# One megakernel of eight stages: layer-norm work of two causal attention stages moved to their beginnings

## The chip, the cores and the metric

One core of a Trainium2 chip. The metric is the device time of one execution in microseconds, from the first to the last instruction of the core and what lies around them; a measurement is the median of several executions. The kernel is one program of 24930 instructions.

## The reference

Four transformer layers on x of 4 sequences x 512 tokens x 128 channels, float32. Each half-layer is `x = x + f(layernorm(x))`:

- L0: gated linear attention; grouped routed experts with a shared expert.
- L1: attention with low-rank q and k factors (16 heads of 8 channels), softmax and a causal mask; routed experts.
- L2: a block whose weights are generated (`tanh(mix) * W + B`): layernorm with gain and bias, causal softmax attention (16 heads of 8), residual, layernorm, a GELU MLP; then a ternary feed-forward `h = silu(x w1 s1) * (x w2 s2)`, two GELU layers 512 to 512, and an output layer.
- L3: full attention (16 heads of 64); dispatched experts with capacity.

The parts that matter here:

```python
def _layernorm(x, axis=-1, eps=1e-05):
    m = jnp.mean(x, axis=axis, keepdims=True)
    v = jnp.var(x, axis=axis, keepdims=True)
    return (x - m) / jnp.sqrt(v + eps)

scores = jnp.einsum('bhqd,bhkd->bhqk', q, k) / float(HD) ** 0.5
scores = jnp.where(causal, scores, -10000.0)
attn = jax.nn.softmax(scores, axis=-1)
```

The L2 block is itself applied to the normalised x, so its residual `hs` is a normalised x too, and its attention normalises twice.

## The kernel before, in words

The residual x stays in SBUF as 16 tiles of 128 tokens x 128 channels. Each sequence is a chunk c (B = 4 chunks, TPC = 4 tiles each). The stages run one after the other, in the order 0 to 7, each in a block of its own; a stage writes out for each of the engines a list of instructions with semaphore waits. Stage 2 is `low_rank_attention` (L1), stage 4 `generated_block` (L2: `generated_attention`, then `generated_mlp`), stage 5 `ternary_ffn`, stage 6 `full_attention`. Projections are made in three matmuls from a high and a low part of weights and rows (fp32r), which add up to float32.

**Layer norm** (class `LayerNorm`) has these steps for a chunk: `stats_of` (VectorE, L200 and L203, 4 tiles each), `rstd_of` (GpSimd, L236 or L239 and the power at L242), `scaled_by` (L214, four tiles of 128x128, on VectorE or GpSimd), `turned` (TensorE, four transposes, L252), `copied` (ScalarE, a high part at L261 or L264 and the float32 copy at L266 or L268) and `low_part_by` (L224, VectorE or GpSimd). The scaled rows have two buffers, so chunk c waits until chunk c-2 was turned.

**The causal stages** (`causal_attention`, stages 2 and 4) work through 16 quads q, four per chunk; a quad is four heads in the four row groups of TensorE. A quad's steps: project q and k (`q`, `k`: L2303 to L2305), make their stacks (`q_stack`, `k_stack`: ScalarE L2418, VectorE L2482), 12 units of scores for the row maxima (`max`: TensorE L2323, VectorE L2502), the maxima turned (`maxT`, L2332) and subtracted (`less`, L2511), scores less the maxima in 6 parts (`exp`, L2344) with their exponentials (`exp_done`, ScalarE L2429 or L2432), a causal cut by GpSimd (L2270), products with the values (`pv`, L2358), and the quotient (`turn`, `norm`). Once a chunk: values (`v`, L2311; `v_done`, L2490) and output (`oT`, `y`). A list written out by hand, `TEMPLATE`, gives the order of one quad's period, with steps of several quads in it (the `pv` of a quad come two periods after its `max`); `causal_plan` unrolls it, and TensorE, ScalarE and VectorE each walk through the same plan and do their part of each item.

PSUM: `p1` two banks for the maxima, `p2` two double banks for the scores, `po` for the products with the values, and `pm`, a single bank, for all odd jobs: q, k, maxT, v, oT, y and, before, the turned rows of chunks 1 to 3 (`ln`). An odd job waits until the one ahead of it in the list was emptied.

**Before the change** a causal stage begins with chunk 0 alone: VectorE makes its statistics, scales its rows, and later makes the statistics of chunks 1 to 3. GpSimd clears the mask and the wide maxima right behind the first deviation (L2234 to L2237), clears the values' tile with its column of ones (L2240, L2242), and scales chunk 1. In the quads, GpSimd's queue holds the cuts of a quad and behind them, at fixed quads, the low part of the next chunk, the scaling of the one after it, and the output's bias added to the residual (L2252); in stage 4 ahead of this the normalised residual of the chunk (`make_hs`, L2616 to L2621). The item `("ln", c)` for chunks 1 to 3 stands behind the fourth unit of maxima of quad 4c-2.

**The ternary stage**: weights are split into 10 pieces of 128x512 (`SplitWeights`: high part on ScalarE, L301; low part on GpSimd, L306). GpSimd's queue: deviation of chunk 0, low part of piece 0, then pieces 1 to 5, then the deviation of chunk 1, then the low parts of the hidden rows. VectorE forms h0 = silu(a) * b in four steps f (L2089) with a high part each (L2082), and scales the next chunk's rows behind the first of them. TensorE's up-projection (L2006 to L2008) for step f waits for h0 of step f-2.

**The full attention stage**: GpSimd clears a tile for the maxima (L2846) and a tile of ones (L2848) around the first deviation.

## Time and profile before

| | us |
|---|---|
| median of 3 executions | 1692.11 |
| lowest and highest | 1687.55, 1694.02 |
| the profiled execution's own time | 1689.31 |
| its span, first to last instruction | 1687.6 |

The profile shows one execution. A row of the timeline gives start, duration, engine, line of the kernel, operation, what is written and read, the count, and in brackets the idle time of the engine before it and who ended it; rows with a count above 1 run several instructions of a kind together. PE is TensorE, PEld its weight loads, DVE VectorE, ACT ScalarE, POOL GpSimd. Rows of matmuls that overlap are pipelined.

Stages in the trace: stage 2 begins at 321 us and ends at 549, stage 4's attention goes from 642 to 868, the ternary stage from 906 to 1062, the full attention from 1062.

### The profile page before, as it was taken

Reading aid. Unit: us, or ns where it says so; the run is one execution under the profiler, and the core shown is the slowest. Engines: PE = TensorE matmul, PEld = TensorE weight load, DVE = VectorE, ACT = ScalarE, POOL = GpSimd, SP = SyncE. Lnnn points to the kernel's source line nnn. Section 1 sums busy time; section 2 is a strip of 40 time slices with the busy share of each in tenths; the row PEclk is TensorE's granted clock in tenths of the full one; section 3 lists DMA queues with packets and bytes.
Section 4 is the critical chain, followed back from the end, with each engine's and each line's share of the span. In section 5 each row is a group of like instructions: output and inputs, shape, how many; then the busy total and the mean of one; then the engine's idle time right before and its main releaser. Section 6 shows DMA issues by size and latency. Waiting matters only on the chain. (4 is left out here: it accounts for less than half of the span.)

```text
span 1687.6 us, 24930 instructions
## 1 busy us (share of the span) xinstructions
PE 1395.5 (83%) x8907; PEld 849.4 (50%) x8907; DVE 1042.6 (62%) x2864; ACT 747.3 (44%) x1169; POOL 763.4 (45%) x833
## 2 busy tenths in 40 slices
PE   5576688789998795999977999899999999985193
PEld 3354566644454562444435777555554545534062
DVE  5766678567884646688833222578778777757112
ACT  4554244336665341566644333455455454430041
POOL 5442344423432555354443442356555455563533
PEclk9688789859999796699978999799999999997597
DMA  3000004200000322000001020000000000003213
GB/s 97 7 8 1 34 22 193 85 1 1 1 2 1 129 63 97 1 2 1 2 0 53 1 100 1 1 1 1 1 1 1 1 1 1 1 1 125 63 51 100
DMA packets 29562, 52.74 MB, mean 31 GB/s; under 512 B 3216, under 2 KB 24592, under 8 KB 27264
## 3 DMA queue, kind: packets, MB, share of 16 engines
q1 hardware_dynamic: 26144, 44.36, 7.5%
q0 software_dynamic: 3296, 6.78, 1.2%
q8 instruction: 73, 1.20, 0.3%
q14 instruction: 49, 0.40, 0.1%
HBM read 29.07 MB, written 21.02 MB: 30 GB/s over the span
## 5 line engine op out<-in xcount | busy, mean ns | idle before, releaser
L2502 DVE CUSTOM_DVE_ANT_0 s_masked_scores<-s_for_max,s_mask_qk 128x128 bf16<-128x128 f32 (+3 forms) x512 | 227.0, 486 | 58.3 <-PE s_for_max L2323 56.4
L2863 POOL TENSOR_TENSOR wbuf<-s_probs 128x1024 f32<-128x1024 f32 x64 | 152.0, 2374 | 201.9 <-ACT s_probs L3022 201.9
L3022 ACT ACTIVATE s_probs<-s_scores 128x1024 f32<-128x1024 f32 x128 | 132.2, 1033 | 202.2 <-PE s_scores L2944 202.2
L2270 POOL TENSOR_SCALAR_AFFINE_SELECT s_probs<-s_probs 128x256 f32<-128x256 f32 x256 | 99.9, 407 | 247.7 <-ACT s_probs L2429 149.6
L3064 DVE TENSOR_REDUCE s_negmax<-s_for_max 128x2 f32<-128x1024 f32 x126 | 152.2, 1208 | 21.4 <-PE s_for_max L2919 21.3
L2323 PE MATMUL s_for_max<-s_k_stack,s_q_stack 32*128 32x128 f32 (+3 forms) x512 | 142.6, 441 | 26.9 <-DVE s_max_wide L2502 17.5
L3071 DVE RECIPROCAL s_recip<-s_pv_and_sums 128x128 f32<-128x128 f32 x128 | 116.6, 934 | 47.3 <-PE s_pv_and_sums L2970 47.3
L2323 PEld LDWEIGHTS s_for_max<-s_k_stack,s_q_stack 32*128 32x128 f32 x512 | 72.3, 205 | 128.8 <-DVE s_max_wide L2502 87.0
L2429 ACT ACTIVATE s_probs<-s_scores 128x1024 f32<-128x1024 f32 x128 | 127.4, 1024 | 14.0 <-PE s_scores L2344 13.7
L2957 PE MATMUL s_pv_and_sums<-s_probs,s_v 128*64 128x512 f32 x512 | 123.9, 605 | 0.9 <-DVE wbuf L3079 0.9
L2358 PE MATMUL s_pv<-s_probs,s_v_and_one 128*32 128x512 f32 (+3 forms) x1024 | 96.9, 474 | 1.5 <-DVE s_o L2521 1.5
L2418 ACT ACTIVATE s_low_rows_hi<-s_odd_jobs,s_low_rows_bias,s_low_rows 128x512 fp32r<-128x512 f32 x64 | 49.8, 777 | 106.9 <-PE s_odd_jobs L2305 106.9
L2344 PE MATMUL s_scores<-s_q_stack,s_k_stack 32*128 32x512 f32 (+3 forms) x512 | 81.8, 396 | 0.7 <-ACT s_probs L2429 0.7
L2868 POOL TENSOR_TENSOR xnT<-wbuf 128x1024 f32<-128x1024 f32 x32 | 78.1, 2442 | 2.5
L1986 POOL TENSOR_TENSOR s_h_lo<-s_h,s_h_hi 128x512 fp32r<-128x512 f32 x32 | 42.3, 1323 | 74.8 <-DVE s_h_hi L2082 74.8
L2944 PE MATMUL s_scores<-s_q_hi,s_k_hi 64*128 64x512 f32 x256 | 64.1, 497 | 9.6 <-ACT s_probs L3022 9.6
L1263 POOL TENSOR_TENSOR s_hidden_lo<-s_hidden,s_hidden_hi 128x512 fp32r<-128x512 f32 x36 | 46.4, 1290 | 46.3 <-ACT s_hidden_hi L1374 46.2
L2944 PEld LDWEIGHTS s_scores<-s_q_hi,s_k_hi 64*128 64x128 f32 x256 | 24.0, 184 | 77.2 <-issue 56.3
L2957 PEld LDWEIGHTS s_pv_and_sums<-s_probs,s_v 128*64 128x64 f32 x512 | 31.2, 136 | 61.4 <-issue 61.4
L2919 PE MATMUL s_for_max<-s_k_hi,s_q_hi 64*128 64x512 f32 x252 | 51.9, 407 | 0.8 <-ACT s_k_hi L2998 0.8
L3220 POOL DMA_INDIRECT expert_rows<-s_y,s_place_int x32 | 30.6, 957 | 47.4 <-DVE s_place_int L3429 37.3
L2944 PE MATMUL s_scores<-s_q_lo,s_k_hi 64*128 64x512 f32 x256 | 51.2, 395 | 0.0
(574 smaller groups left out, 3431.3 us busy)
## 6 DMA issues: line engine op xcount, KB each, us to landing
rows_by_expert<-s_empty_rows SPq DMA_DIRECT2D x8, 1032.0 KB, 10.5
s_w<-extra SPq DMA_DIRECT2D x2, 2048.0 KB, 10.1
wbuf<-w SPq DMA_DIRECT2D x1, 3460.0 KB, 11.2
s_generators<-extra SPq DMA_DIRECT2D x1, 2898.0 KB, 12.8
wbuf<-w SPq DMA_DIRECT2D x1, 2888.0 KB, 9.7
wbuf<-w SPq DMA_DIRECT2D x1, 2124.0 KB, 8.1
dispatched<-s_empty_slots SPq DMA_DIRECT2D x1, 2064.0 KB, 8.5
s_rows<-dispatched SPq DMA_DIRECT2D x8, 258.0 KB, 2.8
```

The lines of the kernel that those rows point to most:

```text
L2270: last = nc.gpsimd.affine_select(out=diag, in_=diag, compare_op=ALU.is_ge, fill=0.0, base=0, pattern=[[0, diag.shape[1]], [1, P]], channel ...
L2323: last = nc.tensor.matmul(p1[m % 2][:, at:at + n], stacks[0][rows, q % SLOTS, i * P:n], stacks[1][rows, q % SLOTS, 0:n], start=True, stop= ...
L2344: last = nc.tensor.matmul(p2[n % 2][:, at:at + S - j * P], stacks[1][rows, q % SLOTS, j * P:(j + 1) * P], stacks[0][rows, q % SLOTS, j * P ...
L2358: last = nc.tensor.matmul(po[32 * x:32 * x + 32, j * P:S], v32[:, c % 2, j, 4 * g + x, :], probs[:, q % 2, slab, at:at + S - j * P], start ...
L2429: nc.scalar.activation(probs[:, q % 2, r, :], p2[n % 2][:, :], ACT.Exp, scale=scale).then_inc(s_exp, 1)
L2502: last = nc.vector.tensor_tensor_reduce(out=junk[:, m % 2, at:at + n], in0=p1[m % 2][:, at:at + n], in1=mask[:, S - n:S], scale=1.0, scala ...
L2863: nc.gpsimd.tensor_tensor(added[half], probs[:, g % 2, 2 * half, :, :], probs[:, g % 2, 2 * half + 1, :, :], ALU.add).then_inc(s_added, 1)
L2944: last = nc.tensor.matmul(p2[:, x, :], kp, qp, start=(part == 0), stop=(part == 3))
L2957: last = nc.tensor.matmul(po[x * dh:(x + 1) * dh, :], v[:, c % 2, j, (2 * n + x) * dh:(2 * n + x + 1) * dh], probs[:, g % 2, j, x, :], sta ...
L3022: nc.scalar.activation(probs[:, g % 2, j, :, :], p2[:, :, :], ACT.Exp, scale=dh ** -0.5).then_inc(s_exp, 1)
L3064: nc.vector.tensor_reduce(negmax[:, g % 2, :, j], max_bank(g, j)[:, :, :], AX.X, ALU.max, negate=True).then_inc(s_neg, 1)
L3071: nc.vector.reciprocal(recip[:, at], ps_sum[:, at]).then_inc(s_rec, 1)
```

## The change

In both causal stages: the rows of all chunks are normalised in the beginning. VectorE makes the statistics of chunk 1 ahead of chunk 0's scaling, those of chunk 2 behind the biases and those of chunk 3 behind the low part of chunk 0. New items `("rows", c)` let VectorE scale chunk 1 ahead of the first q_stack and chunks 2 and 3 behind it. The `ln` items stand behind q(0), k(0) and max(0, 1), and turn into quarters of the score banks `p2` instead of the bank for odd jobs; the first two parts of the scores wait until these are copied out. GpSimd waits for chunk 0's scaled rows before it clears mask and maxima, and for the first two stacks before it clears the values' tile; behind that it makes the low parts of chunks 1 to 3, and adds the bias (stage 2: all chunks; stage 4: two chunks, with their residual). The rest of stage 4's residual is made in single steps, one a quad, behind the first cut of a quad. In the ternary stage the deviation of chunk 1 stands behind the second piece of the split weights. In the full attention stage the tile of ones is cleared ahead of the deviation.

```diff
--- before.py
+++ after.py
@@ -1968,7 +1968,9 @@
             pool.wait_ge(ln.s_xn, TPC)
             split.gpsimd(pool, range(1))
             pool.wait_ge(ln.s_lo, 1)
-            split.gpsimd(pool, range(1, 2 + n))
+            split.gpsimd(pool, range(1, 2))
+            ln.rstd_of(pool, 1)
+            split.gpsimd(pool, range(2, 2 + n))
             for c in range(B):
                 if c == 2 and clear:
                     nc.gpsimd.iota(empty_i[:, :], pattern=[[1, SLOTS7 // P]], base=T,
@@ -1976,7 +1978,7 @@
                     nc.gpsimd.memset(empty[:, :, 0:D], 0.0).then_inc(s_empty, 1)
                     pool.wait_ge(s_empty, 2)
                     nc.gpsimd.tensor_copy(empty[:, :, D], empty_i[:, :]).then_inc(s_empty, 1)
-                if c + 1 < B:
+                if c and c + 1 < B:
                     ln.rstd_of(pool, c + 1)
                 for i, h in enumerate((h0, h1)):
                     if c == 0 and i == 1:
@@ -2168,13 +2170,16 @@
         at = plan.index(item) + 1
         plan[at:at] = more
 
-    for c in range(1, B):
-        behind(("max", QUADS * c - 2, 3), ("ln", c))
+    plan.insert(plan.index(("q", 0)), ("rows", 1))
+    behind(("q", 0), ("ln", 1))
+    behind(("q_stack", 0), ("rows", 2), ("rows", 3))
+    behind(("k", 0), ("ln", 2))
+    behind(("max", 0, 1), ("ln", 3))
     return plan
 
 
 def causal_attention(sh, stage, ctx, ln, probs, p1, p2, po, pm, wst, qk_bias, s_wst, wv, wo, v_bias, o_bias, scale,
-                     before_scalar, before_vector, before_tensor, clear_gpsimd, hs=None, make_hs=None):
+                     before_scalar, before_vector, before_tensor, clear_gpsimd, hs=None, s_hs=None, make_hs=None):
 
 
 
@@ -2212,7 +2217,8 @@
     s_bias = sem("o_bias_added")
     SETUP = 6 + 4
     plan = causal_plan()
-    odd = [item for item in plan if item[0] in ("q", "k", "maxT", "v", "oT", "y", "ln")]
+    odd = [item for item in plan if item[0] in ("q", "k", "maxT", "v", "oT", "y")]
+    turned_in = [None, p2[0][:, 0:S], p2[0][:, S:2 * S], p2[1][:, 0:S]]
     block = ctx.enter_context(nc.Block())
 
     def emptied(item):
@@ -2220,7 +2226,7 @@
         what, n = item[0], item[1]
         if what in "qk":
             return s_stack, 2 * n + "qk".index(what) + 1
-        return {"maxT": s_sub, "v": s_v32, "oT": s_oTs, "y": s_x, "ln": ln.ready}[what], n + 1
+        return {"maxT": s_sub, "v": s_v32, "oT": s_oTs, "y": s_x}[what], n + 1
 
     @block.sync
     def _(sp):
@@ -2230,13 +2236,17 @@
     def _(pool):
         nc.gpsimd.iota(row[:, :], pattern=[[0, 1]], base=0, channel_multiplier=1).then_inc(s_row, 1)
         clear_gpsimd(pool)
-        ln.rstd_of(pool, 0)
+        for c in range(2):
+            ln.rstd_of(pool, c)
+        pool.wait_ge(ln.s_xn, TPC)
         nc.gpsimd.memset(mask[:, :], 0.0).then_inc(s_mask, 1)
         nc.gpsimd.memset(wide[:, :, :, :, :], 0.0).then_inc(s_wide, 1)
         pool.wait_ge(s_mask, 1)
         nc.gpsimd.affine_select(out=mask[:, S - P:], in_=mask[:, S - P:], compare_op=ALU.is_ge, fill=NEG,
                                 base=0, pattern=[[-1, P]], channel_multiplier=1).then_inc(s_mask, 1)
-        ln.rstd_of(pool, 1)
+        for c in range(2, B):
+            ln.rstd_of(pool, c)
+        pool.wait_ge(s_stack, 2)
         nc.gpsimd.memset(v32[:, :, :, :, HD8:32], 0.0).then_inc(s_ones, 1)
         pool.wait_ge(s_ones, 1)
         nc.gpsimd.memset(v32[:, :, :, :, HD8:HD8 + 1], 1.0).then_inc(s_ones, 1)
@@ -2244,18 +2254,21 @@
         resid = sh.x if hs is None else hs
 
         def add_bias(c):
-            if make_hs:
-                make_hs(pool, c)
-            else:
-                pool.wait_ge(ln.s_xn, (c + 1) * TPC)
+            pool.wait_ge(ln.s_xn if s_hs is None else s_hs, (c + 1) * TPC)
             ts = slice(c * TPC, (c + 1) * TPC)
             nc.gpsimd.tensor_tensor(resid[:, ts, :], resid[:, ts, :],
                                     o_bias.unsqueeze(1).broadcast_to([P, TPC, D]), ALU.add).then_inc(s_bias, 1)
 
-        ln.scaled_by(nc.gpsimd, pool, 1)
-        add_bias(0)
-        for c in range(2, B):
-            ln.rstd_of(pool, c)
+        for c in range(1, B):
+            ln.low_part_by(nc.gpsimd, pool, c)
+        if s_hs is None:
+            for c in range(B):
+                add_bias(c)
+        else:
+            for c in range(2):
+                for step in range(1 + TPC):
+                    make_hs(pool, c, step)
+                add_bias(c)
         for q in range(B * QUADS):
             for r in range(EXPS):
                 pool.wait_ge(s_exp, EXPS * q + r + 1)
@@ -2270,13 +2283,12 @@
                     last = nc.gpsimd.affine_select(out=diag, in_=diag, compare_op=ALU.is_ge, fill=0.0, base=0,
                                                    pattern=[[0, diag.shape[1]], [1, P]], channel_multiplier=-1)
                 last.then_inc(s_cut, 1)
-            c = q // QUADS + 1
-            if c < B and q % QUADS == 0:
-                ln.low_part_by(nc.gpsimd, pool, c)
-            if c + 1 < B and q % QUADS == 1:
-                ln.scaled_by(nc.gpsimd, pool, c + 1)
-            if c < B and q % QUADS == 2:
-                add_bias(c)
+                c, step = divmod(q - 1, 2 + TPC)
+                if s_hs is not None and r == 0 and 0 <= c < B - 2:
+                    if step <= TPC:
+                        make_hs(pool, c + 2, step)
+                    else:
+                        add_bias(c + 2)
         if hs is not None:
             for c in range(B):
                 ts = slice(c * TPC, (c + 1) * TPC)
@@ -2339,6 +2351,8 @@
                 pe.wait_ge(s_sub, q + 1)
             if n >= 2:
                 pe.wait_ge(s_exp, n - 1)
+            else:
+                pe.wait_ge(ln.ready, 3 + n)
             for x, j, at in score_units(r):
                 rows = slice(32 * x, 32 * x + 32)
                 last = nc.tensor.matmul(p2[n % 2][:, at:at + S - j * P], stacks[1][rows, q % SLOTS, j * P:(j + 1) * P],
@@ -2401,8 +2415,7 @@
             elif item[0] == "y":
                 project_out(item)
             elif item[0] == "ln":
-                odd_bank(item)
-                ln.turned(pe, item[1], pm)
+                ln.turned(pe, item[1], turned_in[item[1]])
 
     @block.scalar
     def _(act):
@@ -2418,7 +2431,7 @@
                 nc.scalar.activation(low[:, k, :], pm[:, :], ACT.Identity, bias=low_bias[:, k, g:g + 1],
                                      scale=sel[:, k:k + 1]).then_inc(s_low, 1)
             elif item[0] == "ln":
-                ln.copied(act, item[1], pm[:, :])
+                ln.copied(act, item[1], turned_in[item[1]])
             elif item[0] == "exp_done":
                 _, q, r = item
                 n = EXPS * q + r
@@ -2462,20 +2475,20 @@
                 st.did(nc.vector.tensor_scalar(low_bias[:, k, :], bias[:, k, :], sel[:, k:k + 1], None, ALU.mult))
             st.wait()
 
+        ln.stats_of(dve, 1)
         ln.scaled(dve, 0)
         dve.wait_ge(sh.wsem[stage], 16)
         set_bias()
         st.end()
+        ln.stats_of(dve, 2)
         before_vector(dve)
-        ln.stats_of(dve, 1)
         ln.low_part(dve, 0)
-        for c in range(2, B):
-            ln.stats_of(dve, c)
-        dve.wait_ge(s_mask, 2)
-        dve.wait_ge(s_wide, 1)
+        ln.stats_of(dve, 3)
         resid = sh.x if hs is None else hs
         for item in plan:
-            if item[0] in ("q_stack", "k_stack"):
+            if item[0] == "rows":
+                ln.scaled(dve, item[1])
+            elif item[0] in ("q_stack", "k_stack"):
                 q, k = item[1], "qk".index(item[0][0])
                 g = q % QUADS
                 dve.wait_ge(s_low, 2 * q + k + 1)
@@ -2494,6 +2507,9 @@
             elif item[0] == "max":
                 _, q, u = item
                 m = UNITS * q + u
+                if m == 0:
+                    dve.wait_ge(s_mask, 2)
+                    dve.wait_ge(s_wide, 1)
                 dve.wait_ge(s_max, m + 1)
                 if u == 0 and q >= 2:
                     dve.wait_ge(s_maxT, q - 1)
@@ -2610,24 +2626,25 @@
         def first_rows_scalar(act):
             ln.copied(act, 0)
 
-        def make_hs(pool, c):
+        def make_hs(pool, c, step):
             ts = slice(c * TPC, (c + 1) * TPC)
-            pool.wait_ge(ln.s_mv, (c + 1) * TPC)
-            nc.gpsimd.tensor_scalar(rstd[:, ts], ln.mv[:, ts, 1], LN_EPS, 1.0, ALU.add, ALU.mult).then_inc(s_once, 1)
-            pool.wait_ge(s_once, 2 * c + 1)
-            nc.gpsimd.tensor_tensor(rstd[:, ts], rstd[:, ts], sh.mhalf[:, ts], ALU.pow).then_inc(s_once, 1)
-            pool.wait_ge(s_once, 2 * c + 2)
-            for t in range(c * TPC, (c + 1) * TPC):
+            if step == 0:
+                pool.wait_ge(ln.s_mv, (c + 1) * TPC)
+                nc.gpsimd.tensor_scalar(rstd[:, ts], ln.mv[:, ts, 1], LN_EPS, 1.0, ALU.add, ALU.mult).then_inc(s_once, 1)
+                pool.wait_ge(s_once, 2 * c + 1)
+                nc.gpsimd.tensor_tensor(rstd[:, ts], rstd[:, ts], sh.mhalf[:, ts], ALU.pow).then_inc(s_once, 1)
+            else:
+                t = c * TPC + step - 1
+                pool.wait_ge(s_once, 2 * c + 2)
                 nc.gpsimd.tensor_scalar(sh.hs[:, t, :], sh.x[:, t, :], ln.mv[:, t, 0:1], rstd[:, t:t + 1],
                                         ALU.subtract, ALU.mult).then_inc(s_hs, 1)
-            pool.wait_ge(s_hs, (c + 1) * TPC)
 
         ca, cab = gen["ca_w"], gen["ca_b"]
         stacked = [[part[:, k, :, :, :].rearrange("p h r d -> p (h r d)") for part in wst] for k in range(2)]
         causal_attention(sh, stage, ctx, ln, probs, p1, p2, po, pm, stacked, cab[:, 0:2 * QUADS], s_wst,
                          ca[:, 2 * D:3 * D], gen["cp_w"], cab[:, 2 * QUADS:2 * QUADS + D], gen["cp_b"], HD8 ** -0.5,
                          first_rows_scalar, lambda dve: None, first_rows_tensor, lambda pool: None, hs=sh.hs,
-                         make_hs=make_hs)
+                         s_hs=s_hs, make_hs=make_hs)
 
 
 def generated_mlp(sh, stage, hid=512):
@@ -2844,8 +2861,8 @@
 
             pool.wait_ge(sh.wsem[stage], 16)
             nc.gpsimd.memset(negmax[:, :, :, :], 0.0).then_inc(s_const, 1)
+            nc.gpsimd.memset(ones[:, :], 1.0).then_inc(s_const, 1)
             ln.rstd_of(pool, 0)
-            nc.gpsimd.memset(ones[:, :], 1.0).then_inc(s_const, 1)
             pool.wait_ge(ln.s_xn, TPC)
             low_weights(0)
             pool.wait_ge(s_xlo, 1)
```

## Rows read from the trace of the kernel before

**Rows 1.** The page's first part: busy time, share of the span, instructions

```profile
PE 1395.5 (83%) x8907; PEld 849.4 (50%) x8907; DVE 1042.6 (62%) x2864; ACT 747.3 (44%) x1169; POOL 763.4 (45%) x833
```

**Rows 2.** Stretches: length, busy us (instructions) per engine, granted clock, DMA share, GB/s

```profile
321.47:386.32 64.85, 50.86 (x214) 30.87 (x214) 38.87 (x161) 19.25 (x25) 21.36 (x36) 0.50 0.14 56
642.32:703.76 61.44, 44.19 (x154) 24.05 (x158) 38.76 (x160) 19.33 (x24) 24.95 (x40) 0.50 0.12 49
918.80:922.21 3.41, 1.29 (x6) 0.72 (x4) 1.56 (x3) 1.12 (x2) 2.87 (x4) 1.00 0.00 0
922.21:932.46 10.25, 8.34 (x21) 6.33 (x22) 4.35 (x8) 5.12 (x8) 6.63 (x6) 0.50 0.01 2
```

**Rows 3.** Timeline of VectorE, the writes of k_stack: stage 2, then stage 4

```profile
339.25 0.75 DVE L2482 SCALAR_TENSOR_TENSOR s_k_stack<-s_odd_jobs,s_qk_bias,s_low_rows_hi 128x512 fp32r<-128x512 f32 x1 [2.55 <-ACT s_low_rows_hi L2418]
...
351.55 0.75 DVE L2482 SCALAR_TENSOR_TENSOR s_k_stack<-s_odd_jobs,s_qk_bias,s_low_rows_hi 128x512 fp32r<-128x512 f32 x1
...
403.69 0.74 DVE L2482 SCALAR_TENSOR_TENSOR s_k_stack<-s_odd_jobs,s_qk_bias,s_low_rows_hi 128x512 fp32r<-128x512 f32 x1
...
414.07 0.74 DVE L2482 SCALAR_TENSOR_TENSOR s_k_stack<-s_odd_jobs,s_qk_bias,s_low_rows_hi 128x512 fp32r<-128x512 f32 x1
...
426.56 0.75 DVE L2482 SCALAR_TENSOR_TENSOR s_k_stack<-s_odd_jobs,s_qk_bias,s_low_rows_hi 128x512 fp32r<-128x512 f32 x1
...
503.87 0.74 DVE L2482 SCALAR_TENSOR_TENSOR s_k_stack<-s_odd_jobs,s_qk_bias,s_low_rows_hi 128x512 fp32r<-128x512 f32 x1
...
514.87 0.75 DVE L2482 SCALAR_TENSOR_TENSOR s_k_stack<-s_odd_jobs,s_qk_bias,s_low_rows_hi 128x512 fp32r<-128x512 f32 x1
...
731.11 0.74 DVE L2482 SCALAR_TENSOR_TENSOR s_k_stack<-s_odd_jobs,s_qk_bias,s_low_rows_hi 128x512 fp32r<-128x512 f32 x1
...
743.97 0.75 DVE L2482 SCALAR_TENSOR_TENSOR s_k_stack<-s_odd_jobs,s_qk_bias,s_low_rows_hi 128x512 fp32r<-128x512 f32 x1
...
821.63 0.74 DVE L2482 SCALAR_TENSOR_TENSOR s_k_stack<-s_odd_jobs,s_qk_bias,s_low_rows_hi 128x512 fp32r<-128x512 f32 x1
...
832.63 0.74 DVE L2482 SCALAR_TENSOR_TENSOR s_k_stack<-s_odd_jobs,s_qk_bias,s_low_rows_hi 128x512 fp32r<-128x512 f32 x1
```

**Rows 4.** Timeline of TensorE, stage 2: turned rows of chunk 1, then first values products

```profile
368.13 1.12 PE L252 MATMUL s_odd_jobs<-ident,s_ln_xn 128*128 128x128 f32 x4
...
369.18 0.58 PE L2344 MATMUL s_scores<-s_q_stack,s_k_stack 32*128 32x256 f32 x2
...
370.50 2.05 PE L2311 MATMUL s_odd_jobs<-wbuf,xnT 128*128 128x128 f32 x8 [0.74 <-ACT xnT L268]
...
380.53 1.94 PE L2358 MATMUL s_pv<-s_probs,s_v_and_one 128*32 128x512 f32 x8
```

**Rows 5.** Timeline of VectorE, then TensorE, in the beginning of stage 2

```profile
331.46 0.86 DVE L200 BATCH_NORM_STATS2 s_ln_stats<-x_resid 128x6 f32<-128x128 f32 x4
...
332.51 0.66 DVE L224 TENSOR_TENSOR s_xnT_lo<-xnT,s_xnT_hi 128x512 fp32r<-128x512 f32 x1
...
335.95 0.75 DVE L2482 SCALAR_TENSOR_TENSOR s_q_stack<-s_odd_jobs,s_qk_bias,s_low_rows_hi 128x512 fp32r<-128x512 f32 x1 [0.69 <-ACT s_low_rows_hi L2418]
...
341.63 1.40 PE L2323 MATMUL s_for_max<-s_k_stack,s_q_stack 32*128 32x512 f32 x2 [0.79 <-DVE s_max_wide L2502]
```

**Rows 6.** Timeline of VectorE and GpSimd, beginning of stage 4: first rows and a clearing

```profile
645.05 1.92 DVE L214 TENSOR_SCALAR s_ln_xn<-x_resid,s_ln_mv,s_ln_rstd 128x128 f32<-128x128 f32 x4 [0.97 <-POOL s_ln_rstd L242]
...
645.38 0.94 POOL L2235 MEMSET s_max_wide<- 128x1024 f32 x1
```

**Rows 7.** Timeline of the ternary stage: VectorE, GpSimd, VectorE, TensorE

```profile
909.17 1.11 DVE L214 TENSOR_SCALAR s_ln_xn<-x_resid,s_ln_mv,s_ln_rstd 128x128 f32<-128x128 f32 x4 [1.42 <-POOL s_ln_rstd L242]
...
912.84 6.41 POOL L306 TENSOR_TENSOR s_w_lo<-wbuf,s_w_hi 128x512 fp32r<-128x512 f32 x5 [0.62 <-DVE s_xnT_lo L224]
...
920.64 2.05 DVE L214 TENSOR_SCALAR s_ln_xn<-x_resid,s_ln_mv,s_ln_rstd 128x128 f32<-128x128 f32 x4 [2.53 <-POOL s_ln_rstd L242]
...
923.41 0.79 PE L2006 MATMUL s_a<-s_xnT_hi,s_w_hi 128*128 128x512 f32 x1 [3.31 <-DVE s_h L2089]
```

## The prediction

> **What bounds the kernel now.** I read the page first. TensorE is busy for 83% of the span, VectorE for 62% [rows 1], but no engine is busy throughout, so what the change is worth has to be read where it works: the beginnings of the two causal stages (stage 2 from 321 us, stage 4 from 642 us), their quads, and the first chunk of the ternary stage (906 to 935 us).
>
> Then the table of stretches with the granted clock. Both causal stages run their first 64.9 and 61.4 us at 0.50, which is 1.2 GHz, and everything behind that at full clock [rows 2]. TensorE's activity is thin there: 50.9 of 64.9 us, with idle gaps at every handover. The reader should see that each matmul or transpose on the path costs about twice as much in the beginning as later.
>
> Then the timeline of VectorE, cut down to one instruction per quad, the write of k_stack. From one to the next is the period of a quad. A plain quad takes 10.38 us (403.69 to 414.07). A quad that holds a chunk's values and the next chunk's turned rows takes 12.49 us (414.07 to 426.56). The last quad with values has no turned rows behind it and takes 11.00 us (503.87 to 514.87). In stage 4 the same two are 12.86 and 11.00 us [rows 3]. So a chunk of turned rows in mid-plan costs 1.49 us in stage 2 and 1.86 us in stage 4. The reason is the one bank for odd jobs: transposes, ScalarE's two copies out, then the values, then the next projection, all in a line. VectorE sits idle for that line, since it can't take the values before they are made.
>
> **The change, part by part.** No instruction is added or dropped. GpSimd's 24 scalings of 128x128 in the two causal stages become VectorE's, and the rest is order, banks and waits.
>
> *Turned rows out of the quads.* For chunks 2 and 3 the gain is read off directly: 2 x 1.49 = 3.0 us in stage 2, 2 x 1.86 = 3.7 us in stage 4. Chunk 1 stands in the filling of the pipe, at the low clock. There the transposes begin at 368.13, the scores behind them at 369.18, and the values' matmuls at 370.50, after waiting 0.74 us for ScalarE's copy [rows 4]. Without the transposes the scores (0.58 us) start at 368.13 and the values at 368.7: 1.8 us earlier. In stage 4 the copies carry scale and bias and are longer; I add the difference of the later quads, 0.37 us: 2.2 us. Sum of this part: 4.8 + 5.9 = 10.7 us. What is late next is the chain every plain quad has, and the 11.00 us quads show its price, so I expect no new wait. Bounds: all of it, or half of the filling's share, if something else ends last there: 8.7 to 10.7.
>
> *The new beginning, stage 2.* Before, VectorE made the statistics of chunk 1 at 331.46, between the low weights and the low part of chunk 0, which came at 332.51 [rows 5]. After, they are made while it waits for the first deviation, so the low part starts 1.05 us earlier. Behind it stood two sets of statistics; now one set and four scaled rows stand there. A set is about 1.1 us, four rows alone are 1.11 us [rows 7], so q_stack still comes with its 0.69 us to spare [rows 5]. The other eight rows, 2.2 us, go into VectorE's 2.55 us of idle time before k_stack [rows 3]. If that cover were gone, 0.3 us per set would show. TensorE's transposes of chunk 1 and 2 fall into its waits for the stacks. Those of chunk 3 stand between the second and third unit of scores for the maxima, where TensorE is idle 0.79 us [rows 5]; four transposes are 1.12 us [rows 4], so some 0.4 us shows. Stage 2's beginning: 1.0 - 0.4 = 0.6 us gained.
>
> *The new beginning, stage 4.* There are no weights to split, so the low part waits for ScalarE's copies, and these for the first four rows. These took 1.92 us beside GpSimd's clearings (0.94 us for the wide maxima alone) [rows 6], where four rows alone take 1.11 [rows 7]. The clearings now wait for the rows: up to 0.8 us gained. Against it, chunk 1's statistics now precede the rows (about 1.1 us in a gap of 0.97 us [rows 6]: 0.2 us lost), and the clearings fall on the small bias steps and the next statistics, which may hand everything back. Bounds -0.2 to +0.6; I take 0.2, less the 0.4 us of chunk 3's transposes: -0.2.
>
> *GpSimd.* Its queue now stops for chunk 0's rows (behind it: mask, wide maxima, deviations 2 and 3) and for the first two stacks (behind it: the ones column, three low parts, the bias, in stage 4 the normalised residual of two chunks). Who needs them: VectorE's rows 2, the first maxima, the values some 30 us later, the cuts of the first probabilities. GpSimd is busy 21.4 of 64.9 and 25.0 of 61.4 us there [rows 2], so I cost this at nothing; if the cuts came late, the first values product would wait. In stage 4 the residual's steps now stand behind the first cut of a quad; the product that needs the cuts comes a quad later. Nothing.
>
> *Ternary stage.* Five split weights of GpSimd fill 912.84 to 919.25, then comes the second deviation, and VectorE's four rows start only at 920.64, after 2.53 us of idle time [rows 7]; its next gated product is late and TensorE stands still 3.31 us until 923.41 [rows 7]. After: the second weight ends at 914.1, the deviation takes 1.39 us (919.25 to 920.64), the other four weights then end at 916.8, 918.1, 919.4 and 920.6 (1.28 us each). VectorE comes at 918.1, in the midst of them. The rows of stage 4 show that a scaling waits for the GpSimd instruction that is running, but also that two in flight came through behind it (four took 1.92, not one per instruction). So two rows behind 919.4 and two behind 920.6: done at 920.8 instead of 922.69, gain 1.9 us. Bounds: 0.3 if each row waits for an instruction of its own, 3.5 if none waits (918.1 and 1.11 us). The Trainium skill, "SBUF — State Buffer", in "SBUF: two separate sides", says the pair of ports that VectorE and GpSimd share is locked for a whole instruction and the other engine fully blocks. By that rule the lower bound is the one to take, if turns are strict; the rows of stage 4 agree with the blocking and not with strict turns.
>
> *The clock there.* It was high for 3.41 us, of which TensorE worked 1.29 us, then low for 10.25 us with 8.34 us of work [rows 2]. With a gap of 1.4 us in place of 3.3 us I expect it to stay up. The 8.34 us would halve, 4.2 us at most; I take 3.5. Ternary stage: 5.4 us (0.3 to 7.7).
>
> *Last attention stage.* One clearing of 128x64 moves ahead of a deviation that waits for VectorE anyway. Nothing.
>
> **Sum.** Stage 2: 0.6 + 4.8 = 5.4. Stage 4: 5.9 - 0.2 = 5.7. Ternary: 5.4. Together 16.5 us, of an execution of 1689.31 us (span 1687.6): 1672.8. That execution is 2.8 us under the median of 1692.11, so against the median it is 1675.6, 1.0% faster. I say 1675.5.
>
> **Rivals.**
> 1. *The scaled rows take turns with the split weights* in the ternary stage. Speaks for it: 1.92 us in place of 1.11 [rows 6, 7]. Then 0.3 us are left there and the clock falls as before: 11.4 us in all, 1680.7.
> 2. *The low clock ends earlier in the fillings,* since the transposes thicken TensorE's beginning and the gap behind them goes. A quad takes 12.30 us at the low clock (339.25 to 351.55) and 10.38 at the high [rows 3]; one quad fewer in each stage is 3.8 us, with the forecast 1671.7; two quads 1668. Against: in stage 2 it rose at 386.32 [rows 2], 5.8 us after the first values products began (380.53 [rows 4]), the densest work so far.
> 3. *The low clock lasts longer.* The place is the same: TensorE has less work in the quads that used to raise the clock. Each further quad costs 1.9 us. From nine further quads in the two stages together the gain of 16.5 is eaten, and from fourteen it is slower by over 0.5%: 1702. Against: the dense products begin the same number of quads in, and the clock rose at once behind them.
> 4. *The rows delay the first stacks.* VectorE runs in order; if eight rows took 3.8 us like the blocked ones of stage 4, k_stack would slip by 1.3 us in both stages: 1678.1.
>
> **How the numbers follow.** Forecast 0.5, rival 1 0.22, rival 2 0.1, rival 4 0.1, rival 3 0.03, and 0.05 that the mid-plan gain is only partly there (1684 to 1690). A measurement of this kernel can tell about 0.5% (8.5 us) from no change: faster is below 1683.7. The forecast, rivals 1, 2 and 4 lie there, but rival 1 together with rival 4 and the scatter of the runs (1687.55 to 1694.02) reaches the bound, so faster 0.84, same 0.13, slower 0.03. The range goes from two quads of earlier clock (1668) to rivals 1 and 4 together (1683.3), widened below and above by little: 1667 to 1684.
>
> **What would show it.** The k_stack periods: no 12.49 or 12.86 left, 11.00 in their place, plain quads 10.38 as now. k_stack of quad 0 about 1 us earlier after stage 2's beginning, and about as late as now in stage 4. In the ternary stage TensorE's gap of 3.31 us under 1.5, and the clock at 1.00 from there on. Wrong would be: a wait of VectorE's q_stack or k_stack on nothing but its own rows, values products waiting for GpSimd, or periods above 10.4 in plain quads.

## The result and the profile after

| | us |
|---|---|
| before, median of 8 executions (lowest, highest) | 1689.06 (1684.88, 1694.02) |
| after, median of 8 executions (lowest, highest) | 1677.76 (1671.32, 1682.32) |
| ratio after to before | 0.9925, 95% interval 0.9904 to 0.9946 |
| the profiled execution of after: own time, span | 1678.31, 1676.4 |

The changed kernel is faster, by 0.5 to 1.0%. The same program was timed twice more: 0.9891 (0.9863 to 0.992) and 0.9913 (0.9888 to 0.9937). My 1675.5 against 1692.11 is a ratio of 0.9902, which lies in the second and third interval and a little below the first. The total was about right; what it is made of was not.

The page's first part after the change (columns as in [rows 1]):

```profile
PE 1402.2 (84%) x8907; PEld 853.4 (51%) x8907; DVE 1051.3 (63%) x2888; ACT 749.4 (45%) x1169; POOL 745.6 (44%) x809
```

24 instructions went from GpSimd (833 before) to VectorE (2864 before); the other engines have as many as before.

Where the time went, by stage. A stage is counted from its first statistics to the next stage's.

| us | stages 0, 1 | 2 | 3 | 4, attention | 4, MLP | 5, ternary | 6 | 7 |
|---|---|---|---|---|---|---|---|---|
| before | 313.3 | 227.8 | 92.9 | 226.1 | 38.1 | 156.1 | 469.3 | 155.6 |
| after | 313.5 | 221.1 | 92.7 | 222.7 | 38.1 | 156.0 | 469.1 | 156.1 |

The whole gain is in the two causal stages: 6.7 and 3.4 us. The ternary stage gave 0.1 us. (Another 1.5 us lie ahead of the first statistics, in the first loads: 8.4 and 7.0 us. A further trace of the kernel before has 7.6 there, and the changed kernel's other two have 8.4 and 7.9, so that is scatter.)

*The quads.* VectorE's writes of k_stack after, stage 2 and then stage 4, where before had [rows 3]:

```profile
399.18 0.75 DVE L2495 SCALAR_TENSOR_TENSOR s_k_stack<-s_odd_jobs,s_qk_bias,s_low_rows_hi 128x512 fp32r<-128x512 f32 x1
409.54 0.74 DVE L2495 SCALAR_TENSOR_TENSOR s_k_stack<-s_odd_jobs,s_qk_bias,s_low_rows_hi 128x512 fp32r<-128x512 f32 x1
420.54 0.74 DVE L2495 SCALAR_TENSOR_TENSOR s_k_stack<-s_odd_jobs,s_qk_bias,s_low_rows_hi 128x512 fp32r<-128x512 f32 x1
...
709.26 0.74 DVE L2495 SCALAR_TENSOR_TENSOR s_k_stack<-s_odd_jobs,s_qk_bias,s_low_rows_hi 128x512 fp32r<-128x512 f32 x1
721.14 0.74 DVE L2495 SCALAR_TENSOR_TENSOR s_k_stack<-s_odd_jobs,s_qk_bias,s_low_rows_hi 128x512 fp32r<-128x512 f32 x1
732.15 0.75 DVE L2495 SCALAR_TENSOR_TENSOR s_k_stack<-s_odd_jobs,s_qk_bias,s_low_rows_hi 128x512 fp32r<-128x512 f32 x1
```

The plain quad is 10.36 us as before, and the quad with values is now 11.00 us in both stages (409.54 to 420.54, 721.14 to 732.15), where it was 12.49 and 12.86. But 709.26 to 721.14 is a plain quad of 11.88 us. The stretches with their granted clock show why (columns as in [rows 2]; the last two follow on each other):

```profile
320.06:381.50 61.44, 51.54 (x222) 32.18 (x222) 43.00 (x174) 21.61 (x29) 24.13 (x37) 0.50 0.15 59
634.09:692.11 58.02, 45.09 (x162) 25.39 (x166) 41.14 (x172) 22.27 (x28) 31.99 (x47) 0.50 0.13 52
705.99:709.40 3.41, 2.80 (x21) 1.53 (x22) 3.38 (x17) 2.63 (x5) 1.60 (x3) 1.00 0.01 2
709.40:712.81 3.41, 3.41 (x19) 1.38 (x18) 1.70 (x6) 2.08 (x3) 1.17 (x3) 0.50 0.00 0
```

The two fillings still run at 0.50, for 61.4 and 58.0 us instead of 64.9 and 61.4. Then, in the midst of the quads, the granted clock is 1.2 GHz again for 3.41 us, and that quad is 1.5 us longer. I call this a dip. TensorE is busy for all of it, but that is no sign of denser work: its matmuls take longer at the low clock. In the 3.41 us ahead of the dip it had worked 2.80 us. A second one fell into stage 4's last quad with values (12.42 instead of 11.00 us).

*The filling of stage 2.* TensorE after, the place of [rows 4]:

```profile
365.08 0.87 PE L2335 MATMUL s_for_max<-s_k_stack,s_q_stack 32*128 32x512 f32 x2
365.17 0.58 PE L2358 MATMUL s_scores<-s_q_stack,s_k_stack 32*128 32x256 f32 x2
366.02 2.05 PE L2323 MATMUL s_odd_jobs<-wbuf,xnT 128*128 128x128 f32 x8
```

Scores, beside the scores for the maxima (L2335), then at once the values (L2323), with no transposes and no wait of 0.74 us for a copy. TensorE before, the row just ahead of [rows 4]:

```profile
367.28 0.87 PE L2323 MATMUL s_for_max<-s_k_stack,s_q_stack 32*128 32x512 f32 x2
```

*The beginning of stage 2.* VectorE, then GpSimd and TensorE:

```profile
330.19 0.68 DVE L224 TENSOR_TENSOR s_xnT_lo<-xnT,s_xnT_hi 128x512 fp32r<-128x512 f32 x1
...
333.55 0.75 DVE L2495 SCALAR_TENSOR_TENSOR s_q_stack<-s_odd_jobs,s_qk_bias,s_low_rows_hi 128x512 fp32r<-128x512 f32 x1 [0.61 <-ACT s_low_rows_hi L2431]
334.22 2.13 DVE L214 TENSOR_SCALAR s_ln_xn<-x_resid,s_ln_mv,s_ln_rstd 128x128 f32<-128x128 f32 x8
336.86 0.75 DVE L2495 SCALAR_TENSOR_TENSOR s_k_stack<-s_odd_jobs,s_qk_bias,s_low_rows_hi 128x512 fp32r<-128x512 f32 x1 [0.51 <-ACT s_low_rows_hi L2431]
...
337.67 2.66 POOL L2250 MEMSET s_v_and_one<- 128x3072 f32 x1 [4.35 <-DVE s_k_stack L2495]
...
338.39 1.11 PE L252 MATMUL s_scores<-ident,s_ln_xn 128*128 128x128 f32 x4
```

Both stacks still wait for ScalarE (0.61 and 0.51 us), so the rows are hidden. The eight rows of chunks 2 and 3 take 2.13 us in the gap ahead of k_stack. Chunk 3's transposes (L252) start at 338.39, behind the first scores for the maxima. GpSimd stands still 4.35 us until the stacks are written and then clears for 2.66 us.

*The beginning of stage 4*:

```profile
637.11 1.08 DVE L214 TENSOR_SCALAR s_ln_xn<-x_resid,s_ln_mv,s_ln_rstd 128x128 f32<-128x128 f32 x4
...
638.52 0.55 POOL L2242 MEMSET s_mask_qk<- 128x512 f32 x1
639.01 0.97 POOL L2243 MEMSET s_max_wide<- 128x1024 f32 x1
```

The first rows take 1.08 us instead of 1.92 [rows 6], and the clearings come behind them.

*The ternary stage.* VectorE, its rows by form (shortest, median, longest in ns), GpSimd, TensorE:

```profile
906.74 4.02 DVE L214 TENSOR_SCALAR s_ln_xn<-x_resid,s_ln_mv,s_ln_rstd 128x128 f32<-128x128 f32 x4
...
L214 DVE TENSOR_SCALAR s_ln_xn<-x_resid,s_ln_mv,s_ln_rstd x4: 335/1304/1316, 906.7 to 910.4; 128x128 f32<-128x128 f32 x4
...
904.02 5.18 POOL L306 TENSOR_TENSOR s_w_lo<-wbuf,s_w_hi 128x512 fp32r<-128x512 f32 x4
...
911.48 0.80 PE L2008 MATMUL s_a<-s_xnT_hi,s_w_hi 128*128 128x512 f32 x1 [2.83 <-DVE s_h L2091]
```

The rows start right behind the first step, without the 2.53 us of idle time, as wanted, but take 4.02 us instead of 2.05 [rows 7]: three of them 1.3 us each, one behind each of GpSimd's subtractions, the fourth 0.34. TensorE's gap is 2.83 us, from 3.31. And the clock:

```profile
897.13:907.37 10.24, 6.95 (x18) 5.23 (x19) 5.89 (x20) 5.42 (x9) 8.22 (x8) 0.50 0.57 212
907.37:910.78 3.41, 1.27 (x6) 0.69 (x4) 3.41 (x5) 1.07 (x2) 3.05 (x3) 1.00 0.00 0
910.78:921.02 10.24, 8.83 (x22) 6.69 (x23) 3.86 (x6) 5.12 (x8) 7.12 (x6) 0.50 0.01 2
```

Up for 3.4 us, in which TensorE worked 1.27, then down for 10.24 us: the picture of [rows 2].

### The profile page after: what moved, and what is told of

It is laid out like the page before. It is cut to its first block and busy times, and to the rows that moved or that the text cites. A ratio compares the mean times of both kernels' runs of the same rounds, so it can differ in the third digit from the quotient of the medians.

```text
span 1676.4 us, 24921 instructions
## 1 busy us (share of the span) xinstructions
PE 1402.2 (84%) x8907; PEld 853.4 (51%) x8907; DVE 1051.3 (63%) x2888; ACT 749.4 (45%) x1169; POOL 745.6 (44%) x809
## 5 line engine op out<-in xcount | busy, mean ns | idle before, releaser
L2335 PE MATMUL s_for_max<-s_k_stack,s_q_stack 32*128 32x128 f32 (+3 forms) x512 | 143.4, 446 | 23.6 <-DVE s_max_wide L2518 16.0
L2335 PEld LDWEIGHTS s_for_max<-s_k_stack,s_q_stack 32*128 32x128 f32 x512 | 72.5, 206 | 126.0 <-DVE s_max_wide L2518 85.5
L2974 PEld LDWEIGHTS s_pv_and_sums<-s_probs,s_v 128*64 128x64 f32 x512 | 31.2, 136 | 61.4 <-issue 61.4
```

The source lines that it names most:

```text
L2335: last = nc.tensor.matmul(p1[m % 2][:, at:at + n], stacks[0][rows, q % SLOTS, i * P:n], stacks[1][rows, q % SLOTS, 0:n], start=True, stop= ...
L2974: last = nc.tensor.matmul(po[x * dh:(x + 1) * dh, :], v[:, c % 2, j, (2 * n + x) * dh:(2 * n + x + 1) * dh], probs[:, g % 2, j, x, :], sta ...
```

## The experiments

In the first set each part was put into the kernel before by itself (e1, e2), the ternary stage's blocking was taken away (e3), and the changed kernel ran again (e4).

**e1** and **e2**, the parts alone. e1 is the kernel before with this, and e2 the kernel after without it:

```diff
-            split.gpsimd(pool, range(1, 2 + n))
+            split.gpsimd(pool, range(1, 2))
+            ln.rstd_of(pool, 1)
+            split.gpsimd(pool, range(2, 2 + n))
...
-                if c + 1 < B:
+                if c and c + 1 < B:
```

> The kernel before with the ternary stage's part of the change alone. Forecast's theory: 1.9 us from the rows and 3.5 us from the clock, about 5.4 us faster than the kernel before (0.3%). Theory of turns (each scaled row waits for one whole GpSimd subtraction, as the changed kernel's trace shows with three rows of 1.31 us): 0.1 to 0.5 us, which no timing tells from nothing; the trace has three long rows, a gap of TensorE of about 2.8 us, and the clock falls as before. If the ternary part only looked idle in one profile by chance, the times would differ by several us.

> The changed kernel with the ternary stage as before. Theory of turns: the whole gain of about 0.7% stays here, ratio to the kernel before 0.992 to 0.994. Forecast's theory: the ternary part carried a third, so the ratio would be about 0.9955. In the trace the steady quads of both causal stages are 10.37 us, those with values 11.00, with or without the two dips of the clock that the changed kernel's stage 4 had; dips at other quads, or none, speak for chance, dips at the same two quads for a cause in the plan.

Measured: e1 0.9985 (0.997 to 0.9999), e2 0.988 (0.9853 to 0.9906). So the causal part makes the gain. The ternary part by itself gave 0.2 to 5.1 us, by its interval little or nothing, and the forecast's 5.4 lies just outside it. In e1 the rows took 4.01 us in the same turns. Its stage 5 was 153.2 us all the same, 2.9 below before, since the low clock behind the gap lasted 3.4 us in this trace and not 10.2. Against that stand two dips in stage 4, with the old causal plan (quads of 11.89 and 11.85 us). e2's stage 2 took 221.3 us and its stage 4 220.1, without a dip.

**e3**, early rows that nothing blocks. Chunk 1's rows stand ahead of the first step, and GpSimd holds pieces 2 to 5 back until they are written:

```diff
             ln.rstd_of(pool, 1)
+            pool.wait_ge(ln.s_xn, 2 * TPC)
             split.gpsimd(pool, range(2, 2 + n))
...
             ln.stats_of(dve, 1)
+            ln.scaled(dve, 1)
...
-                    if f == 0 and c + 1 < B:
+                    if f == 0 and c and c + 1 < B:
```

> The changed kernel, but VectorE scales chunk 1 of the ternary stage ahead of h0(0), and GpSimd holds pieces 2 to 5 of the split weights until these rows are done. Theory of turns: the rows take 1.1 us in VectorE's idle time, h0(1) then waits for ScalarE alone, TensorE's gap of 2.83 us shrinks to about 0.5 us; 2.5 to 3 us gained from that against the changed kernel. If a short gap keeps the clock up, 3 us more, 5 to 6 us in all. Rival: the clock falls all the same, or pieces 4 and 5 become late and the first hidden layer waits for GpSimd instead: under 2 us.

**e4**, the kernel after:

> The changed kernel once more, for a second trace. Theory: the two dips of the clock in stage 4 (quads of 11.88 and 12.42 us) come from where the chip's clock decisions fall against the thin part of a quad, so they sit elsewhere or are missing, and spans differ by 1.5 us per dip. Rival: stage 4's changed queue of GpSimd delays something at these quads; then they come again at the same quads.

Measured: e3 0.9897 (0.9876 to 0.9919), span 1668.7; e4 0.9891, span 1672.7. By time the two can't be told apart. The traces can: e3's rows took 1.11 us, its clock stayed at 1.00 behind the first 10.24 us, and stage 5 took 151.2 us. In e4 the rows took the same 4.02 us as in after, and yet the clock stayed up in this execution. TensorE's gap and the stretches in e4:

```profile
910.45 0.50 PE L2008 MATMUL s_a<-s_xnT_hi,s_w_hi 128*128 128x512 f32 x1 [3.08 <-DVE s_h L2091]
```

```profile
905.79:909.20 3.41, 1.59 (x7) 0.94 (x5) 3.41 (x4) 1.38 (x2) 3.41 (x3) 1.00 0.00 0
909.20:919.40 10.20, 7.82 (x35) 6.26 (x36) 4.92 (x9) 5.70 (x9) 7.93 (x7) 1.00 0.01 2
```

The stage took 152.5 us where after took 156.0. In the same stretch behind the first 10.24 us at the low clock, TensorE had worked 1.59 us here and 1.27 us in after. The same program thus has both outcomes, and the clock alone is worth 3.5 us here. Rows without turns add 1.3 us to that (152.5 to 151.2).

The second set has one trace each of four kernels and no interval. **e5**, the kernel before:

> The kernel before once more, for a second trace. If the clock's falls in quads and in the ternary stage are a matter of where its decisions fall, then this trace differs from the first in such places: a quad of 11.8 to 11.9 us somewhere, or the ternary stage at another length than 156.1 us, with nothing changed in the program. Rival: stage lengths repeat within 0.3 us, and the changed kernel's differences of 3 us are the change's.

Measured: span 1685.7, no dip, every quad's period of [rows 3] within 0.02 us, stage 5 156.0 us.

**e6**, GpSimd's clearings without their two waits:

```diff
-        pool.wait_ge(ln.s_xn, TPC)
...
-        pool.wait_ge(s_stack, 2)
```

> The changed kernel without GpSimd's two new waits (chunk 0's scaled rows, first two stacks), so that its clearings stand where they did. Theory: they block VectorE's scaling again: first four rows of stage 4 about 1.9 us instead of 1.1, its k_stack(0) 0.6 to 1 us later counted from the first statistics; stage 2 nearly the same, since its weights end last, unless the column of ones (2.7 us) falls on the rows of chunk 1 and delays q_stack by up to 2 us. Rival: the new order alone carries the gain and the waits carry nothing: both stages unchanged within 0.2 us.

Measured: first rows unchanged (1.08 us in both stages): the deviation of chunk 1, which the change put ahead of the clearings, keeps GpSimd busy until VectorE is done, so the first wait costs and saves nothing. The second one matters. VectorE in stage 2 of e6, then GpSimd:

```profile
333.35 4.38 DVE L214 TENSOR_SCALAR s_ln_xn<-x_resid,s_ln_mv,s_ln_rstd 128x128 f32<-128x128 f32 x8
337.65 0.73 DVE L2493 SCALAR_TENSOR_TENSOR s_k_stack<-s_odd_jobs,s_qk_bias,s_low_rows_hi 128x512 fp32r<-128x512 f32 x1
...
332.39 2.66 POOL L2248 MEMSET s_v_and_one<- 128x3072 f32 x1
335.11 0.35 POOL L2250 MEMSET s_v_and_one<- 128x128 f32 x1
335.34 1.28 POOL L224 TENSOR_TENSOR s_xnT_lo<-xnT,s_xnT_hi 128x512 fp32r<-128x512 f32 x1
```

Eight rows take 4.38 us beside the clearings and the low part behind them instead of 2.13, k_stack waits for them instead of for ScalarE, and comes 1.66 us later than in after (18.01 against 16.34 us from the stage's first statistics), in stage 4 1.89 us later. That is my rival 4, and the wait on the two stacks is what prevents it.

**e7**, chunk 3's turned rows back in mid-plan, in the bank for odd jobs, behind the fourth maxima of quad 10, and GpSimd's low part of it (in lines not shown) behind the first cut of quad 9:

```diff
-    behind(("max", 0, 1), ("ln", 3))
+    behind(("max", QUADS * 3 - 2, 3), ("ln", 3))
```

> The changed kernel with chunk 3's turned rows back in mid-plan in the bank for odd jobs (its scaling stays in the beginning, its low part goes behind the first cut of quad 9). Theory: one quad of each stage, from k_stack 10 to 11, takes 12.49 and 12.86 us again instead of 11.00, 1.5 + 1.9 us longer; k_stack 0 to 1 goes from 12.49 back to 12.30. Rival: the cost in mid-plan came from GpSimd's scaling and bias in its queue and not from the bank: then it stays near 11.0.

Measured, k_stack in stage 4 of e7 around that quad:

```profile
762.86 0.75 DVE L2499 SCALAR_TENSOR_TENSOR s_k_stack<-s_odd_jobs,s_qk_bias,s_low_rows_hi 128x512 fp32r<-128x512 f32 x1
775.72 0.75 DVE L2499 SCALAR_TENSOR_TENSOR s_k_stack<-s_odd_jobs,s_qk_bias,s_low_rows_hi 128x512 fp32r<-128x512 f32 x1
```

12.86 us again, and 12.49 in stage 2 with a dip of 1.24 on top (13.73). The other quads with values stay at 11.00. So each 1.49 and 1.86 us belongs to its own chunk's transposes. The first quad's period, where chunk 3's transposes had stood, hardly moved: 12.46 and 12.44 in the two stages instead of 12.49 and 12.50, and 12.30 before. I had costed those transposes at 0.4 us; they cost 0.04.

**e8**, the statistics back behind the first rows (chunk 1 behind the weights, chunk 2 behind the low part of chunk 0; GpSimd's deviation of chunk 1, not shown, goes back behind the mask):

```diff
-        ln.stats_of(dve, 1)
         ln.scaled(dve, 0)
         dve.wait_ge(sh.wsem[stage], 16)
         set_bias()
         st.end()
-        ln.stats_of(dve, 2)
         before_vector(dve)
+        ln.stats_of(dve, 1)
         ln.low_part(dve, 0)
+        ln.stats_of(dve, 2)
         ln.stats_of(dve, 3)
```

> The changed kernel with the statistics of chunks 1 and 2 back behind the weights (chunk 1 ahead of chunk 0's low part, chunk 2 behind it). Theory: in stage 2 the low part and k_stack(0) come 1.0 to 1.1 us later, and with two sets of statistics and four rows before q_stack another 0.4 to 1.1 us; in stage 4 chunk 1's statistics fall in a wait, so 0.4 to 1.1 us from the second set only, less 0.2 us since the first rows start earlier. Rival: other things end last there and nothing moves by more than 0.3 us.

Measured, VectorE in stage 2 of e8, then of e3, which has the changed kernel's causal stages:

```profile
329.53 0.66 DVE L224 TENSOR_TENSOR s_xnT_lo<-xnT,s_xnT_hi 128x512 fp32r<-128x512 f32 x1
...
333.20 0.74 DVE L2494 SCALAR_TENSOR_TENSOR s_q_stack<-s_odd_jobs,s_qk_bias,s_low_rows_hi 128x512 fp32r<-128x512 f32 x1
...
320.69 0.87 DVE L200 BATCH_NORM_STATS2 s_ln_stats<-x_resid 128x6 f32<-128x128 f32 x4 [0.32 <-PEq L1173]
...
329.09 0.68 DVE L224 TENSOR_TENSOR s_xnT_lo<-xnT,s_xnT_hi 128x512 fp32r<-128x512 f32 x1
...
332.44 0.75 DVE L2497 SCALAR_TENSOR_TENSOR s_q_stack<-s_odd_jobs,s_qk_bias,s_low_rows_hi 128x512 fp32r<-128x512 f32 x1 [0.62 <-ACT s_low_rows_hi L2433]
```

From the low part to q_stack it is 3.67 us instead of 3.36, and q_stack no longer waits for ScalarE: with two sets of statistics in front, four rows don't fit. q_stack came 0.2 us late in both stages (13.25 against 13.03 us from the first statistics, 9.54 against 9.31). The low part itself was not later than in after (9.58 against 9.68), but the clocks differ: it fell 1.40 us behind the first statistics in e8 and 0.23 us ahead of them in after. In e3 it fell 1.45 us behind them, as in e8 but for 0.05 us, and there the low part came at 8.40, q_stack at 11.75 and k_stack at 15.06 us, against 9.58, 13.25 and 16.54 in e8. So with the clock alike, the statistics' new place is worth 1.18 us at the low part, where I had 1.05, and 1.5 us at both stacks.

The third set asked whether e3's clock was luck, and whether the early place or the held GpSimd made it. **e9** is e3 again, **e10** the kernel after, **e11** is e9 without `pool.wait_ge(ln.s_xn, 2 * TPC)`:

> The kernel of e3 a second time: chunk 1's rows of the ternary stage scaled ahead of the first h0, GpSimd holding its pieces back until they are done. Theory (the clock there goes by TensorE's gap, and rows that nobody blocks close it): rows about 1.1 us, no TensorE gap over 1.5 us up to the second chunk, granted clock 1.00 behind it, stage 5 about 151 us instead of 152.5 to 156; against the kernel after on the same chip 1.5 to 4.5 us faster, which is 0.1 to 0.3% and at the edge of what timing can tell. Rival (chance: the clock is drawn anew in each execution, and e3 had a lucky one): low clock in the stage again, 155 to 156 us, and timing equal to the kernel after.

> The changed kernel again, beside e9. Stage 5 at 156 us (low clock behind the gap of 2.8 us) or near 152.5 (high); both have been seen, and this says only how often. Rows of chunk 1 take strict turns with the split pieces again (three of 1.31 us). Zero to two clock dips of 3.4 us in the causal quads, 1.5 us each. Span 1671 to 1678.

> e9 without GpSimd's wait: the rows still stand ahead of the first h0, but GpSimd's pieces 2 to 5 run on beside them. If turns are strict, the rows take 3 x 1.31 + 0.33 = 4.3 us again, the first h0 comes about 2 to 3 us later than in e9 and the stage loses what the early place gave: stage 5 at 153 us or more, with a gap of TensorE ahead of the gated product. If what helped in e3 was the early place alone, stage 5 is near 151 as in e3.

Measured: e9 0.9898 (0.9877 to 0.9919), e10 0.9913 (0.9888 to 0.9937), e11 0.9901 (0.9874 to 0.9929). Stage 5: 151.3, 156.0 and 153.7 us. The stretches of e9, and then of e11:

```profile
900.27:910.51 10.24, 6.67 (x17) 5.06 (x18) 6.46 (x23) 5.13 (x9) 6.99 (x7) 0.51 0.57 212
910.51:920.80 10.29, 7.87 (x33) 5.41 (x32) 4.47 (x7) 7.06 (x11) 10.29 (x9) 1.00 0.01 2
```

```profile
906.69:910.10 3.41, 0.62 (x3) 0.50 (x3) 3.38 (x5) 0.69 (x1) 2.13 (x3) 0.99 0.00 0
910.10:913.51 3.41, 3.41 (x9) 2.62 (x9) 2.09 (x3) 0.69 (x1) 2.51 (x2) 0.51 0.02 5
```

And the rows with GpSimd's pieces in e11, by form and in the timeline:

```profile
L214 DVE TENSOR_SCALAR s_ln_xn<-x_resid,s_ln_mv,s_ln_rstd x4: 1300/1303/1321, 903.9 to 907.5; 128x128 f32<-128x128 f32 x4
...
903.79 4.97 POOL L306 TENSOR_TENSOR s_w_lo<-wbuf,s_w_hi 128x512 fp32r<-128x512 f32 x4
```

Four rows, four pieces, one row to a piece: 1.30 us each instead of some 0.28. The early place without the hold thus only moves the gap (TensorE stands 2.79 us ahead of the gated product), and the clock falls behind it. With the hold it did not, in either of two traces. In the timing these kernels overlap with the changed one, so I don't claim a better version; the traces say that e3's order is worth 1.3 to 4.8 us of its stage.

## Why the prediction was right, and where it was not

| us | forecast | measured in the traces |
|---|---|---|
| stage 2, beginning | 0.6 | 1.2 (1.9 where the clock fell later), less 0.2 in the first quad |
| stage 2, filling quad | 1.8 | 2.27 (15.85 to 13.58) |
| stage 2, chunks 2 and 3 | 2 x 1.49 | 2 x 1.49 |
| stage 4, beginning | -0.2 | 0.9, less 0.2 in the first quad |
| stage 4, filling quad | 2.2 | 2.64 (16.22 to 13.58) |
| stage 4, chunks 2 and 3 | 2 x 1.86 | 2 x 1.86, less 2.9 for two dips in after |
| ternary, rows | 1.9 | 0.5 at the gated product, 0.1 in the stage |
| ternary, clock | 3.5 | 0 or 3.5 |

*Turned rows out of the quads*: right, and shown by e7 for one chunk. The filling was sized 0.5 and 0.4 us too low. In stage 2 the trace shows where the rest lies: I let the scores start where the transposes had stood, behind the end of the matmuls for the maxima, so the values 1.4 us behind the start of those (367.28 to 368.7). In after the scores run beside them, 0.09 us behind their start, and the values follow at 0.94 us (365.08 to 366.02), in stage 4 as well (675.13 to 676.07). From the first k_stack to the last, stage 2 went from 175.6 to 170.4 us, stage 4 from 176.7 to 170.5 in the traces without a dip (e2, e8): 5.2 and 6.2, where I had 4.8 and 5.9. And the low clock does not double a matmul's time on this path, as "about twice as much" had it: four transposes took 1.12 us in the filling and 0.66 in a later quad of before, the eight matmuls for the values 2.05 and 1.13.

*The beginnings*: better than forecast, by two steps that I had too dark. "Some 0.4 us shows" for chunk 3's transposes: e7 says 0.04. The first quad did grow by 0.19 us, 0.15 of which stayed in e7, so it isn't these transposes. Nor is it GpSimd's clearing of 2.66 us, which runs just there in after: in e6 it was over before k_stack, and the first quads took 12.47 and 12.48 us. The 0.15 lies between TensorE's first scores for the maxima and VectorE's first maxima (337.66 to 338.64, where before had 340.06 to 340.88), and its cause stays open. In stage 4 I took 0.2 us of the 0.8 that shorter rows could give, since the clearings behind them might hand it back, and they did not. The first rows began at 2.81 us from the first statistics against 2.67 before, so chunk 1's statistics did cost 0.14 us, near the 0.2 I gave them, and ended at 3.89 against 4.59: 0.70 of the 0.84 us that they were shorter came through. The low part came 0.83 us sooner and k_stack 0.93.

Stage 2's beginning also goes by where the clock falls in it, which I had not seen. With the old plan k_stack came at 17.55 us where it fell ahead of the first statistics (before, e5) and at 16.79 where it fell 2.03 us behind them (e1); with the new plan at 16.34 to 16.35 (after, e2, e10, e11) and, again at 2.03 us, 14.86 (e4).

*GpSimd at nothing*: right. TensorE's weight loads waited for its cuts for 2.2 us in all in after and 1.9 in before, and a plain quad's period is 10.36 us in both.

*The ternary stage* is where the prediction failed, in the step "so two rows behind 919.4 and two behind 920.6". I had taken it from stage 4, where four rows beside GpSimd took 1.92 us. There the neighbours were clearings; beside the split weights each row waits for one whole subtraction. The sentence beside my sum, that by the rule in the Trainium skill, "SBUF — State Buffer", "SBUF: two separate sides", the lower bound is the one to take, was the better guide, and every trace of this stage agrees: 1.30 us a row in turns, 0.28 without. The clearings of e6 show the same lock (8 rows, 4.38 us). So rival 1 held for the rows, and in the traces of after, e7, e8 and e10 for the clock as well.

*The clock there*: its size was right, its certainty wrong. Where it stays up, the stage is 3.5 us shorter (e4 against after, one program). With the changed order it fell for 10.2 us in four traces (after, e7, e8, e10: 155.8 to 156.0 us) and for 3.4 us or not at all in three (e1, e6: 153.2 and 153.4 us; e4: 152.5); with the old order it fell in three of three (before, e2, e5: 156.0 to 156.2). Whether the change shifts these odds can't be told from so few.

*Low clock in the fillings*: 3.4 us shorter in each stage, but the clock rose about as many quads in as before; rival 2 did not come as I had it, and rival 3 not either. A piece of rival 2 came in three of ten traces: in e6, e9 and e11 the clock rose earlier in one of the two stages for 3.4 us, fell again for 6.8, and that quad took 12.23 to 12.29 us instead of 13.58.

*The dips* were in no step. The changed causal plan had 0 to 2 in a trace (none in e2; one in e4 and e8; two in after, e3, e6, e7, e9, e10, e11), the old plan none in two traces (before, e5) and two in the third (e1). At 1.2 to 1.5 us each they explain why after's stage 4 gained 3.4 us and e2's 6.0. TensorE had worked 2.8 us in the 3.41 us ahead of every one of these 18 dips. Other stretches of 3.41 us in the quads were as thin or thinner, down to 2.56 us in before, and had no dip behind them, so thin work stands ahead of a dip but does not make one by itself. That they occur with the old plan shows that the change isn't needed for them; that a denser plan draws more of them isn't excluded by three traces, and would have eaten some 1 to 2 us of the gain.

*The total.* Of my 16.5 us, 11.1 were causal and 5.4 ternary. The traces show 12.5 us in the two causal stages without a dip (e2: 6.5 and 6.0), less what dips take, and 0.1 to 3.6 us in the ternary stage. (e2 gave 1.1 us back behind stage 4's last k_stack, 37.0 us against 35.9, at a mean clock of 0.84 against 0.89; e8 took 35.9 there and its stage 4 gained 6.9.) So the causal part came out 1.4 us above its forecast and the ternary part mostly didn't come. The total is right in part by luck: what the causal part gave above its forecast made up for some of what the ternary part lacked, and by what happened in the first trace rival 1, with 11.4 us in all, is the better account. The three timings of the changed kernel put the gain at 12.7, 18.5 and 14.7 us by their ratios. The lower end is what the traces show; e2's timing, 20.3 us, is 7.8 more than its trace has in the stages that were changed. Some of that is the choice of executions: the traced one of before took 1689.3 us, where the median of its set with e2 is 1693.2, and the traced one of e2 took 1678.4, with a median of 1674.2. What made the others different is in executions that no trace shows, and it stays open.

## What to carry to other kernels

Read what a step costs in a pipeline from the period with it against the same period without it: 12.49 against 11.00 forecast its removal to the hundredth. Before VectorE's work is put beside GpSimd's, look which kind stands there: here it advanced one row per GpSimd subtraction of 128x512, however short its own were, and lost nothing beside a power of 128x4. A wait that holds GpSimd back can be worth more than an earlier start: 151.2 us with it (e3) against 153.7 without (e11). A gain that hangs on the granted clock in one place is a chance and not a term: the same program came out 3.5 us apart there, so give it a probability, not a value.
